# A hand-ordered lead-in re-sequenced: norm through two PSUM banks, values turned before query products, outputs interleaved with FFN tiles

## The reference

```python
x = x + _L0_conv_ref(_ln_c(x), ...)      # deformable attention
t = _to_tokens(x)
t = t + _L0_ffn_ref(_ln_t(t), ...)       # 4 experts, top 2, gelu
x = _from_tokens(t, x)
x = x + _L1_conv_ref(_ln_c(x), ...)      # sum of depthwise convolutions, 7x7 in all
t = _to_tokens(x)
t = t + _L1_ffn_ref(_ln_t(t), ...)
```

```python
o = jax.nn.gelu(layernorm(off) * ln_g + ln_b, approximate=False)
pos = jnp.tanh(jnp.einsum('bhwc,pc->bhwp', o, w_off2) + ref)
v_sampled = _grid_sample_bilinear(value, pos[..., ::-1])
attn = jnp.einsum('bcm,bcn->bmn', query, key) * SCALE
out = jnp.einsum('bmn,bcn->bcm', attn, v_sampled)
y = jnp.einsum('bchw,oc->bohw', out, w_out)
```

## Time and profile before

| | us |
|---|---|
| median of 3 runs | 1663.65 |
| lowest and highest | 1660.79, 1666.19 |
| the profiled execution | 1665.84 |
| its span | 1664.0 |
| busy: PE, DVE, ACT, POOL | 1482.3, 918.6, 734.9, 251.8 |
| mean granted TensorE clock | 0.953 |

### The profile page before, as it was taken

One profiled execution on the slowest core, in us unless ns is written; L12 is line 12 of the kernel. 1 busy time (PEld: TensorE's weight loads), 2 busy tenths in 40 slices (PEclk: granted clock), 3 DMA queues, 4 the chain that ended last, 5 costly groups with the idle time before them and its releaser, 6 DMA issues.

```text
span 1664.0 us, 20112 instructions
## 1 busy us (share of the span) xinstructions
PE 1482.3 (89%) x6400; PEld 1004.8 (60%) x6400; DVE 918.6 (55%) x2543; ACT 734.9 (44%) x1534; POOL 251.8 (15%) x190
## 2 busy tenths in 40 slices
PE   3785878988779999988889999999999999998998
PEld 2563655555555676655555677667676776665565
DVE  3836869578994554469994543443434443344323
ACT  3732154246442444445442444453535443355443
POOL 2051325011360000011270000010001000000000
PEclk9986878999899999999899999999999999999999
DMA  3342045134334222333153212352145212320211
GB/s 101 61 128 88 26 99 130 56 107 113 81 81 124 61 77 70 87 99 99 44 137 95 84 60 56 100 139 60 44 98 144 64 46 57 85 67 27 76 58 46
DMA packets 169099, 136.29 MB, mean 82 GB/s; under 512 B 115008, under 2 KB 163010, under 8 KB 168610
## 3 DMA queue, kind: packets, MB, share of 16 engines
q1 hardware_dynamic: 164018, 129.74, 28.6%
q0 software_dynamic: 3072, 4.82, 1.2%
q10 hardware_dynamic: 1904, 0.43, 0.1%
HBM read 95.30 MB, written 39.13 MB: 81 GB/s over the span
## 4 chain that ended last, share of the span: by engine, by line
PE 52%; issue 11%; DVE 10%; ACT 5%; POOL 5%; SPq 2%; DMA 2%; ACTq 0%; POOLq 0%; DVEq 0%
PE y_ps L1052 20%; PE at_ps L1197 9%; PE h_ps L1060 5%; PE h_ps L1061 5%; PE h_ps L1059 5%; POOL pix_mem L958 4%; PE at_ps L1117 3%; DVE vq_mem L1375 3%; ACT ln_cen L773 2%; PE lb_ps L1029 2%; PE lg_ps L1042 1%; POOL ln_rstd L945 1%; DVE part L1331 1%; ACT hidden L898 1%; DMA gate_t<-gates_dram 1%
## 5 line engine op out<-in xcount | busy, mean ns | idle before, releaser
L898 ACT ACTIVATE hidden<-h_ps,b 128x448 f32<-128x448 f32 x672 | 424.6, 635 | 725.8 <-PE h_ps L1061 715.2
L1052 PE MATMUL y_ps<-hidden,w 128*96 128x448 f32 x1344 | 638.6, 560 | 33.3 <-ACT hidden L898 26.9
L1059 PE MATMUL h_ps<-xh,w1h 96*128 96x448 f32 x672 | 475.0, 707 | 1.3 <-ACT pix_mem L818 1.3
L1331 DVE SCALAR_TENSOR_TENSOR part<-y_ps,b,gate_t 96x448 f32<-96x448 f32 x224 | 151.8, 678 | 518.1 <-PE y_ps L1052 479.1
L945 POOL TENSOR_TENSOR ln_rstd<-ln_ve,minus_half 112x4 f32<-112x4 f32 x112 | 148.0, 1321 | 1147.1 <-DVE ln_ve L1314 1137.6
L1052 PEld LDWEIGHTS y_ps<-hidden,w 128*96 128x96 f32 x1344 | 206.8, 167 | 108.9 <-ACT hidden L898 66.6
L1060 PE MATMUL h_ps<-xl,w1h 96*128 96x448 f32 x672 | 250.7, 373 | 0.0
L1061 PE MATMUL h_ps<-xh,w1l 96*128 96x448 f32 x672 | 248.8, 370 | 0.0
L1059 PEld LDWEIGHTS h_ps<-xh,w1h 96*128 96x128 f32 x672 | 130.9, 195 | 140.6 <-issue 123.9
L1060 PEld LDWEIGHTS h_ps<-xl,w1h 96*128 96x128 f32 x672 | 131.8, 196 | 120.9 <-issue 120.0
L773 ACT ACTIVATE ln_cen<-ln_cen,ln_rstd 112x96 f32<-112x96 f32 x448 | 130.2, 363 | 100.0 <-POOL ln_rstd L945 100.0
(11 more groups left out here) (155 smaller groups left out, 1371.3 us busy)
## 6 DMA issues: line engine op xcount, KB each, us to landing
gate_t<-gates_dram SPq DMA_DIRECT2D x112, 336.0 KB
value_pairs<-pix_mem SPq DMA_DIRECT2D x56, 168.0 KB, 3.2
x_mem<-norm_c SPq DMA_DIRECT2D x16, 420.0 KB, 4.3
ln_x<-in_x SPq DMA_DIRECT2D x28, 168.0 KB
res_mem<-in_x SPq DMA_DIRECT2D x4, 1176.0 KB
x_attn<-res_mem SPq DMA_DIRECT2D x16, 294.0 KB, 2.7
res<-x_attn SPq DMA_DIRECT2D x28, 168.0 KB
x_ffn<-ffn_out SPq DMA_DIRECT2D x28, 168.0 KB, 2.0
```

Of the source, the lines that this page charges most:

```text
L898: act.activation(hidden[c % HID_RING][:, :], h_ps[c % H_BANKS][:, 0:TILE], ACT.Gelu, bias=b1[l][:, c:c + 1]).then_inc(gelu_done, 1)
L1052: pe.matmul(y_ps[e % Y_BANKS][0:C, 0:TILE], w2[l][:, c, :], hidden[c % HID_RING][:, :], start=(j == 0), stop=(j == CPE - 1)).then_inc(hid_ ...
L1059: pe.matmul(ps, hi, xh[:, ring(k)], start=True, stop=False)
L1331: dve.scalar_tensor_tensor(part[:, e, :], y_ps[e % Y_BANKS][0:C, 0:TILE], b2[l][:, e:e + 1], gate_t[e // 2][0:C, e % 2, :], ALU.add, ALU.m ...
```

## The change

The tables of the lead-in are written anew; the FFN slots from step (0, 3) on are untouched.

- Steps: `LEAD` is 15, not 13. Images 0 and 1 are both normed from the start, with image 1's tiles 1 to 3 before image 0's stage 0 (which moves from step 4 to 5). Image 2's tiles 3 and 4 and the FFN tiles 5 and 6 come into the lead-in; in steps (0, 0) to (0, 2) only image 2's tiles 5 and 6 are left.
- Two banks: until the first FFN tile, odd jobs are turned to `lg_ps`, even ones to `lt_ps` (`turn_bank`), and a turn waits only for the job before in the same bank. The second turn of a step stands at place 6, not 8, and ACT's second `apply` at 8, not 9.
- Value turned ahead: the third group of the first query products moves behind the turns of value (`QUERY_CONV`), and `offsets` stands behind `combine2`.
- Outputs: Y0 to Y7 are spread over steps 11 and 12, between FFN tiles (`LEAD_Y`, `LEAD_ADD`).
- `expand_w_out` moves from the end of step 8 to that of step 4, `fold_taps` from 8 to 9, the split of `w1` from 9 to `combine0` of 11.
- Gates of the first four tiles are read and made within step 14, the others' within (0, 0), each a step earlier in the count.
- In the lead-in, after a second `normalize` with taps following, DVE waits until POOL has made `ln_rstd`.
- Loads: four small weight loads go from SP's queue to ACT's, the clearing of borders moves behind the first stores, and ACT loads its function table by a dummy instruction before the first tile.

```diff
-LEAD = 13
+LEAD = 15
...
-              (-1, 3): [("a0", 6), ("a1", 0)], (-1, 6): [("a1", 1), ("a1", 2)], (-1, 7): [("a1", 3), ("a1", 4)],
...
+              (-1, 3): [("a0", 6), ("a1", 0)], (-1, 4): [("a1", 1), ("a1", 2)], (-1, 5): [("a1", 3)],
...
+              (-1, 13): [("f0", 3), ("f0", 4)], (-1, 14): [("f0", 5), ("f0", 6)], (0, 0): [("a2", 5)],
+              (0, 2): [None, ("a2", 6)]}
...
+LEAD_Y = {(11, 5): 0, (11, 6): 1, (11, 7): 2, (11, 9): 3, (12, 0): 4, (12, 3): 5, (12, 7): 6, (12, 9): 7}
...
+        QUERY_CONV = {(1, 3): (0, 0), (1, 5): (0, 1), (2, 10): (0, 2), (3, 8): (1, 0), (3, 10): (1, 1), (4, 3): (1, 2)}
...
+        def turn_bank(n):
+            return lg_ps if n < first_f and n % 2 else lt_ps
+
+        def same_bank(n):
+            return max([m for m in range(n) if turn_bank(m) is turn_bank(n)], default=-1)
...
+                for dst, src in tap_rows[:4]:
+                    load(dst, src)
+            act.wait_ge(pool_set, 1)
+            act.activation(g_p[0][:, 0, 0:1], zeros[0:SUB, 0:1], ACT.Copy, scale=1.0)
...
-                if n > 0:
-                    pe.wait_ge(ln_centered, n)
+                if same_bank(n) >= 0:
+                    pe.wait_ge(ln_centered, same_bank(n) + 1)
...
+                    if (slot, p, name) == (-1, 11, "combine0"):
+                        split_weights(0)
...
                         normalize(jobs[1])
+                        if slot < 0 and ops:
+                            dve.wait_ge(ln_scale, jobs[1].n + 1)
...
-                if (slot, p) == (-1, 9):
-                    split_weights(0)
...
-                if (slot, p) == (-1, 8):
+                if (slot, p) == (-1, 4):
                     expand_w_out()
+                if (slot, p) == (-1, 9):
                     fold_taps()
```

More of the change, by code:

```diff
@@ L101 @@
 GATE_TILES = ((0, 4), (4, TILES))
-GATE_STEP = {(-1, LEAD - 1): (0, 0), (0, 1): (0, 1),
+GATE_STEP = {(-1, LEAD - 1): (0, 0), (0, 0): (0, 1),
              **{(slot, TILES - 2 + part): (slot + 1, part) for slot in range(SLOTS - 1) for part in range(2)}}
-GATE_TURN = {after: GATE_STEP[step] for step, after in zip(STEPS, STEPS[1:]) if step in GATE_STEP}
+GATE_TURN = {after: GATE_STEP[step] for step, after in zip(STEPS, STEPS[1:]) if step in GATE_STEP and after != (0, 0)}
+GATE_TURN[-1, LEAD - 1] = 0, 0
 def ffn_slot(slot):
@@ L718, in _ @@
                 if (slot, p) == (-1, 0):
[L719 removed]
+                    zero_pads("a")
                 if (slot, p) == (-1, 1):
@@ L905, in _ @@
                     for job in JOBS[slot, p]:
-                        if slot < 0 and c == LEAD_APPLY[job.place] or slot >= 0 and c == APPLY and job.place == 0:
+                        if slot < 0 and c == (LEAD_APPLY[job.place] if p != 7 else 8) or slot >= 0 and c == APPLY and job.place == 0:
                             apply(job)
@@ L909, in _ @@
                             move(job)
-                    if (slot, p) == (-1, 3) and c == 10:
-                        for g in range(G):
-                            make_diag("off", g)
-                    if (slot, p) == (-1, 4) and c in (1, 3, 6):
-                        make_diag("query", (1, 3, 6).index(c))
-                    if (slot, p) == (-1, 4) and c in (8, 9, 10):
-                        make_diag("key", c - 8)
+                    if slot < 0 and (p, c) in DIAG_AT:
+                        make_diag(*DIAG_AT[p, c])
                     for b, stage in stages:
                         attention(b, stage, c)
-                    if (slot, p) in GATE_STEP and c == (8, 10)[GATE_STEP[slot, p][1] or GATE_STEP[slot, p][0] == 0]:
+                    if (slot, p) in GATE_STEP and c == (8, 10)[GATE_STEP[slot, p][1]]:
                         exp_scores(*GATE_STEP[slot, p])
-                    if (slot, p) in GATE_TURN and c == 3:
+                    if (slot, p) in GATE_TURN and c == (3 if slot >= 0 else 10):
                         take_gates(*GATE_TURN[slot, p])
@@ L1148, in attention @@
                         turn_off(b, ((0, 1), (8, 10))[b].index(c))
-                    if (b, stage) in ((0, 1), (0, 3)) and c in (3, 5, 8):
-                        tap_conv(b, "query", stage // 2, (3, 5, 8).index(c))
-                    if stage == 2 and c in ((10, 10, 11), (0, 1, 2))[b]:
-                        for g in range(G):
-                            if ((10, 10, 11), (0, 1, 2))[b][g] == c:
-                                tap_conv(b, "key", 0, g)
+                    if b == 0 and (stage, c) in QUERY_CONV:
+                        tap_conv(b, "query", *QUERY_CONV[stage, c])
+                    if (b, stage, c) in KEY_CONV:
+                        tap_conv(b, "key", 0, KEY_CONV[b, stage, c])
                 if stage == 2 and TURNS <= c < TURNS + VBLK:
@@ L1218, in _ @@
                     for job in JOBS[slot, p]:
-                        if c == (TURN_IN if slot >= 0 else LEAD_TURN_IN)[job.place]:
+                        if c == (LATE_TURN.get((slot, p), TURN_IN[1]) if job.place else TURN_IN[0]):
                             turn_in(job)
@@ L1226, in _ @@
                         attention(b, stage, c)
-                    if (slot, p) in GATE_TURN and c == 2:
+                    if slot < 0 and (p, c) in LEAD_Y:
+                        times_query(0, LEAD_Y[p, c])
+                    if (slot, p) in GATE_TURN and c == (2 if slot >= 0 else 9):
                         turn_gates(*GATE_TURN[slot, p])
@@ L1644, in _ @@
                             sample_row(b, 1)
-                    if 6 in by_stage:
+                    if slot < 0:
+                        for y in LEAD_ADD.get((p, name), ()):
+                            add_y(0, y)
+                    if (slot, p, name) == (-1, 11, "combine0"):
+                        split_weights(0)
+                    if 6 in by_stage and slot >= 0:
                         for y in Y_BEFORE.get(name, ()):
```

55 lines of the change are left out of this document (30 added, 25 removed), and 5 rows, old and new, of the table START_JOBS.

## The result

The changed kernel takes 1675.22 us (median of 5 runs, 1667.42 to 1677.91) against 1663.65 (median of five as well): a ratio of 1.0066, 95% interval 1.0037 to 1.0094. It is slower, where 1650.7 was forecast.

The account below looks back on a forecast made before the run. It took the lead-in as a chain of hand-overs bound by no engine, with DVE busiest in the three steps. +3.5 for the lead-in and -16.5 for the steps made -13.0, from 1663.65 to 1650.7; range 1638 to 1664.

Parts of the forecast that it names:

- that on value: Lead-in, image 0: taps end at 72.7, last value copy at 82.8, first gather leaves at 91.9, 7.1 early.
- the pricing of a held power at 6: Image 1's two first-tile powers under taps, priced by earlier rows of 6.16 and 5.93 against 1.01 alone.
- the sum's line on this wait: DVE's new wait for POOL's power costs 1.01 to 3.93, taken as 1; 5 us spared to the tile.
- First tiles: Start of lead-in: two banks cut a pair from 8.73 to 5.9, third pair 7 us early; taps start at 47.4.
- Value, sampling, outputs, first gelu: Lead-in marks: first gather 91.9, sampled values complete 140.3, Y0 149.1, first gelu 232.0, which is 3.5 late.
- hidden by them: Lead-in: the fold, 5.09 and about 1 more, sits beside the first gathers and is hidden by them.
- Steps (0, 0) to (0, 2): First gelu to Y0 of image 1: 53.9 instead of 70.5; the three steps give -16.5 in the sum.
- Rest, loads, dummy: Rest keeps its old 1336; moved loads and the dummy instruction cost 0, between -0.5 and +1.
- Faster still: Rival: powers under taps held for one tap only, or ACT's queue not the chain; -17 to -22, say 1644; chance 0.19.
- The banks don't pay: Rival: loads come one after another, third pair starts late, 7 us lost; -6, 1657.7; chance 0.10.
- Gathers become the bound: Rival: image 1's 16 gathers stay slow, Y0 of image 1 at 296.5; -2.4, 1661; chance 0.13.
- The clock falls: Rival: PE pauses in the three steps, places of 1.35 about 1.24 longer; +9 at 24 places, about 1672; chance 0.09.

Follow-up runs that it names:

- e2: Changed kernel plus one DVE wait for POOL's `ln_rstd` before the taps of step (-1, 5): 1662.53 us, ratio 0.9971 to the kernel before.
- e3: Changed kernel plus that DVE wait after every first tile of a lead-in step with taps: 1658.98 us, ratio 0.9949 to the kernel before.
- e4: Changed kernel without the waits it has after second tiles: 1673.17 us, ratio 1.0031 to the kernel before.
- e7: e3 with all turns in one bank again: 1658.94 us, ratio 0.9947 to the kernel before.
- e12: e3 with the folding of tap weights moved behind the split of `w1` in step (-1, 11): 1654.42 us, ratio 0.9926 to the kernel before.
- e5: Changed kernel, no wait added, one small one-input DVE instruction among the 16 taps of step (-1, 5): 1661.84 us, ratio 0.9968 to the kernel before.
- e8: e3 with POOL's power ahead of image 1's first four gathers in step (0, 0), DVE waiting for it: 1658.61 us, ratio 0.9945 to the kernel before.

## Why the prediction was wrong

**The step that failed**: that on value, with its words "the norms of image 1's first tiles are out of the way", and the pricing of a held power at 6. The tile of step (-1, 5) is a first tile, the new wait does not cover it, and 16 taps follow it without a break. The prediction named such a tile ("the first tile of a step is not") and priced only image 1's two. This one cost 17.40, of which 13.99 was ACT idle; undone by one wait it gives 10.5 us (e2), with the later first tiles 14.1 (e3). The 6.16 and 5.93 of the earlier trace rows were taken as a price of the place. They were the length of what was left of a run: at 170.61 an output was added (its input in PSUM) and at 187.40 a one-input tap began, and each power ended within a us of that. The length of the taps up to the next instruction of another kind is the price, here 1.5 up to the first and 16 x 0.94, and 0.9 to end: it could have been counted. The other half of the sum's line on this wait, "against it stand 5 us spared to the tile", failed too: without the waits nothing was longer by more than 0.02 there (e4), as a split stands in between.

**First tiles**: right in size (5.9, the turn at 24.00, taps at 47.7), wrong in cause. The second bank did not do it (e7); the place of the turn did, as far as the order tells. What the text calls the third pair is the fourth, which started at 30.79 before.

**Value, sampling, outputs, first gelu**: with the power mended (e3) the first gather is 1.3 late of the forecast, sampling's end at 140.34 and Y0 at 148.94 within 0.2, the first gelu 1.8 early. The walk through the queues was sound. But "hidden by them" was wrong of the folding: it lay on the path (e12). The end of the sampling came out right all the same (140.34 for 140.3), so the walk's times must carry it, though the text does not show where.

**Steps (0, 0) to (0, 2)**: 61.8 in e3 for 53.9. DVE is busy 51.4 of them, where 59.7 less the 11.4 subtracted for moved work was 48.3: a part of the positions slid behind the gelu, and image 1's first gather leaves 2.5 behind it in e3, 1.1 before. The rest is idle time. The 7.55 before the first combine did go (no wait at 249.43 in the changed kernel), but 6.28 came before the third (7.89 in e3), since image 2's tile had its power behind four gathers, one of them held 4.71 by taps. A wait took the place of the one removed, and the prediction had no rival for that. Together the two stretches from Y0 of image 0 to Y0 of image 1 take 143.0 in e3 and 141.8 before: tiles moved from one to the other brought nothing in sum, and the whole gain of e3 lies ahead of Y0 of image 0.

**Rest, loads, dummy**: its length stayed within what executions of one program differ by (1334.5 to 1341.4), which is more than the forecast's bounds for all the small edits.

**Rivals.** *Faster still* rested on a power getting in behind one tap: refuted, by e5 most directly. Where a single tap was beside it a power did take 2.03 (255.39 in the change), but under a run it waited for all of it. *The banks don't pay* is true of the banks (e7), not of its cause, as the fourth pair started at 24.00; yet a turn did wait 4.53 for its load, at 36.38, and the text had no price for that. *Gathers become the bound* holds as soon as the wait ahead of it is cut (e8). *The clock falls* did not happen in the three steps (0.94 granted, 0.86 before); its 1.24 a place is also more than its own rows give, since 1.25 for 0.71 makes 1.35 about 1.0 longer. The slower side came by a mechanism that the text had in its rows, and only looked at from the side on which it would cost less than 6.

What stays open: how the port is kept over the run (held or taken again each time), why a power gets in between two `TENSOR_TENSOR` and never between two taps, why the load at 36.38 comes where it does and what an earlier one is worth, and why the granted clock differs in the untouched rest.

## What to carry to other kernels

Before putting a long run of back-to-back `SCALAR_TENSOR_TENSOR` with two SBUF inputs on VectorE behind something that GpSimd must still do, count the run: the GpSimd instruction can wait for all of it, and everything in the queues behind it too. Here a wait of 0.66 (e2), or one instruction of 0.17 of another kind in the middle (e5), bought 10 us back. When a resource and an order are changed together, undo them singly before crediting one; and place side work by the idle row on its own engine just ahead of the path's next step, not by the engine that it runs beside.
